# GpSimd's gathers of edge rows no longer wait for TensorE's sums of dense chunks

## The reference, cut to what matters

```python
# x (6250, 64) f32, src/dst/edge_type_32 (200000,) i32, edge_weight (200000,) f32
h_src = x[src]                                    # layer 0: 32 relation types over 4 bases
msg = einsum('ebo,eb->eo', einsum('ei,bio->ebo', h_src, weight), w_comp[etype]) * edge_weight[:, None]
x1 = layernorm(x + relu(segment_sum(msg, dst, 6250) + bias0))
# layer 1: self loops of weight 1, each edge scaled by 1 / (sum of weights at its destination)
norm = deg_inv[dst] * ew
y = segment_sum(norm[:, None] * (x1 @ W)[src], dst, 6250) + b
out = layernorm(x1 + y)
```

## Time and profile before

| | |
|---|---|
| three timed executions | 2766.74, 2771.0, 2766.0 us; median 2766.74 |
| profiled execution, first to last instruction (span) | 2042.2 us |
| profiled execution's own time around its span | not given by the page |
| median less span | 724.5 us |
| mean granted TensorE clock | 0.867 of full speed |
| busy, of the span | PE 73%, GpSimd 73%, VectorE 63%, ScalarE 42% |
| gathers (L824) | 1559, 947 ns each |

### The profile page before, as it was taken

How to read it: one execution, slowest core, us unless ns; L and a number is a source line. 1 busy time by engine, 2 the same in 40 slices (tenths; PEclk the granted TensorE clock), 3 DMA queues, 4 the chain that set the end, 5 groups by cost and what they waited for, 6 DMA issues and landing times.

```text
span 2042.2 us, 61156 instructions
## 1 busy us (share of the span) xinstructions
PE 1497.4 (73%) x21470; PEld 1196.1 (59%) x21470; DVE 1288.6 (63%) x3623; ACT 856.8 (42%) x2171; POOL 1495.6 (73%) x1590
## 2 busy tenths in 40 slices
PE   3785566655765776777677687778778788888986
PEld 2554444544554655566566566566667667677854
DVE  8886555756557555666655575565765656477647
ACT  5563343534444443444344344443444434344313
POOL 7777777777777777777777777777777777777750
PEclk7898777878787888888888898899999999899998
DMA  5544434434334455445444545554355554455695
GB/s 135 156 148 149 141 103 142 140 128 134 92 128 140 121 152 156 147 128 152 142 121 136 147 107 160 148 151 142 105 155 157 165 163 110 122 179 141 198 346 187
DMA packets 197569, 299.93 MB, mean 147 GB/s; under 512 B 66502, under 2 KB 137083, under 8 KB 191135
## 3 DMA queue, kind: packets, MB, share of 16 engines
q1 hardware_dynamic: 99496, 167.96, 23.3%
q0 software_dynamic: 50112, 51.41, 12.9%
q10 hardware_dynamic: 47671, 76.76, 12.4%
HBM read 187.43 MB, written 108.56 MB: 145 GB/s over the span
## 4 chain that ended last, share of the span: by engine, by line
PE 33%; POOL 29%; issue 19%; DMA 9%; DVE 3%; ACTq 3%; ACT 2%; DVEq 1%; POOLq 1%
POOL gathered_rows L824 29%; DMA gathered_rows<-in_x,idx 8%; PE coefs_ps L1383 4%; PE types_ps L1259 4%; PE coefs_ps L1349 3%; PE node_ps L1259 3%; PE sums_ps L1259 3%; PE sums_ps L1283 3%; PE dense_ps L1259 3%; PE sums_ps L1296 3%; ACTq L648 2%; ACT room L1056 1%; PE node_ps L1269 1%; PE sums_ps L1360 1%; PE coefs_ps L1244 1%
## 5 line engine op out<-in xcount | busy, mean ns | idle before, releaser
L824 POOL DMA_INDIRECT gathered_rows<-in_x,idx x1559 | 1475.7, 947 | 477.5 <-issue 426.7
L1283 PE MATMUL sums_ps<-gathered_rows,chunk_factors 128*32 128x64 f32 x3118 | 98.3, 253 | 407.0 <-DMA gathered_rows<-in_x,idx 218.7
L1897 DVE TENSOR_TENSOR first_room<-first_room,dve_ps 128x1024 bf16<-128x1024 bf16 x585 | 365.0, 679 | 0.0
L1283 PEld LDWEIGHTS sums_ps<-gathered_rows,chunk_factors 128*32 128x32 f32 x3118 | 63.1, 125 | 423.2 <-issue 208.6
L1056 ACT COPY room<-dense_ps 128x294 f32 x390 | 168.8, 433 | 332.1 <-PE dense_ps L1259 277.5
L985 ACT COPY parts<-sums_ps 128x128 f32<-128x128 f32 x196 | 52.0, 265 | 465.6 <-PE sums_ps L1283 462.3
L1919 DVE TENSOR_TENSOR dve_ps<-coefs_ps,edges 128x32 f32<-128x32 f32 x196 | 38.6, 197 | 330.7 <-PE coefs_ps L1244 326.2
L1259 PE MATMUL dense_ps<-first_room 128*128 128x245 bf16 x1170 | 219.2, 301 | 31.8 <-DVE first_room L1897 31.6
L1056 ACT COPY room<-node_ps 128x294 f32 x390 | 168.8, 433 | 168.1 <-PE node_ps L1259 61.8
L1891 DVE TENSOR_TENSOR first_room<-dve_ps,first_room 128x1960 bf16<-128x1960 f16 (+2 forms) x260 | 238.7, 939 | 0.0
L1259 PE MATMUL sums_ps<-first_room 128*128 128x245 bf16 (+1 forms) x1170 | 233.8, 312 | 0.0
(11 more groups left out here) (300 smaller groups left out, 2470.4 us busy)
## 6 DMA issues: line engine op xcount, KB each, us to landing
acc_room<-block_table ACTq DMA_DIRECT2D x147, 374.5 KB
block_table<-room SPq DMA_DIRECT2D x11, 2621.5 KB
type_rows<-in_edge_type SPq DMA_DIRECT2D x260, 96.0 KB
gathered_rows<-in_x,idx POOLq DMA_INDIRECT x1559
block_table<-room SPq DMA_DIRECT2D x9, 2247.0 KB
block_table<-room SPq DMA_DIRECT2D x9, 1872.5 KB
block_table<-room SPq DMA_DIRECT2D x10, 1498.0 KB
acc_room<-block_table ACTq DMA_DIRECT2D x43, 321.0 KB
```

What stands on the lines that cost most here:

```text
L824: pool.indirect_dma_start(gathered_rows[:, s, j, 0:D], None, rows, bass.IndirectOffsetOnAxis(ap=idx[:, s, j:j + 1], axis=0)).then_inc(rows ...
L1283: last = nc.tensor.matmul(parts_ps[lane:lane + LANE, D * k:D * k + D], chunk_factors[:, q, c, :], rows, start=True, stop=True)
L1897: last = nc.vector.tensor_tensor(lo_hot[:, w, q0:q1, :, :], lo_hot[:, 2, q0:q1, :, :], part_of_weights(w), ALU.mult)
```

## The change

The table of the awaited counts, the waits with their increments, and the parameter that turned them on go. Everything else stays, the wait for `idx_ready` at the head of each group too.

```diff
-GATHERED_BEHIND = {2: 5, 4: 8, 6: 9}
...
-assert 2 * FETCHES > FIRST_REGULAR + 1 and max(GATHERED_BEHIND.values()) <= 2 * CH
...
-        gathers_paced = sem("gathers_paced")
...
-            def gather_group(step, s, chunks, rows, behind_dense=False):
+            def gather_group(step, s, chunks, rows):
 
                 pool.wait_ge(idx_ready, step + 1)
 
                 pool.sem_inc(gathers_begun, 1)
                 for j in range(chunks):
-                    if behind_dense and j in GATHERED_BEHIND:
-                        pool.wait_ge(dense_summed, step * CH + (FREE_HOTS - CH + GATHERED_BEHIND[j]))
-                        pool.sem_inc(gathers_paced, 1)
                     pool.indirect_dma_start(gathered_rows[:, s, j, 0:D], None, rows,
...
-                        gather_iter(m, v, but_one if v == FETCHES - 1 else whole, True)
+                        gather_iter(m, v, but_one if v == FETCHES - 1 else whole)
...
-                        gather_group(i * U + s, s, CH, x[:, :], True)
+                        gather_group(i * U + s, s, CH, x[:, :])
```

More of the change, by code:

```diff
@@ L834, in _, with gather_iter @@
             with pool.If(early == 1):
-                def gather_iter(m, v, chunks, behind_dense=False):
+                def gather_iter(m, v, chunks):
                     for s in range(U):
-                        gather_group(m * (FETCHES * U) + (v * U + s), s, chunks[s], x[:, :], behind_dense)
+                        gather_group(m * (FETCHES * U) + (v * U + s), s, chunks[s], x[:, :])
                 whole, but_one = (CH, CH, CH), (CH, CH, CH - 1)
```

## The result

The changed kernel takes 3056.14 us (median of 4, 3053.12 to 3057.91), the kernel before 2766.55 us: ratio on record 1.1035, 95% interval 1.1015 to 1.1055 (the two medians alone give 1.105). The prediction said 2766.7 us and gave a tenth to everything outside 2761 to 2772 us. The profiled execution of the changed kernel takes 3057.1 us in all and its span is 3055.3 us, so only 1.8 us lie around the span.

The account below looks back on a forecast made before the run. The prediction took GpSimd's rate of gathers, one every 1.25 us, as the bound, with TensorE waiting for it. Its terms, 0 + 0 + 0 + 0, left the time at 2766.7 us, range 2761.0 to 2772.0.

Parts of the forecast that it names:

- the 724.5 us: Excess of the timed median, 2766.74 us, over the first profile's span, 2042.2 us; left unexplained.
- Slower TensorE work could make them hold: GpSimd's waits might hold in timed executions if TensorE ran slower inside the span; still priced at nothing.
- gathers that go earlier are merely early: If waits held, TensorE would be the bound, so releasing GpSimd's gathers sooner would change nothing: 0 us.
- Steps 1 to 3: GpSimd's 513 waits hold nothing, have time to spare, and their instructions hide in the gather gap: 0 us each.
- the 5.7 us to spare at the tightest place: Gather 1434, gather 6 of its group: its awaited dense chunks were done 5.7 us before it started.
- Step 3: Waits, increments and register arithmetic between GpSimd's gathers are covered by the 0.305 us gap: 0, at most 4.7 us gained.
- Step 4, contention,: GpSimd's gathers meeting VectorE's one-hot building: no stall in the rows, so no term, despite a rule allowing up to 679 ns.
- A: Faster: gaps named after TensorE are the waits' own, or waits hold when timed; 43.6 us gained, 2723.1 us, chance 0.06.
- B: Slower: gathers let loose collide with SyncE's dense block stores and land late; 19 us, 2785.5 us, chance 0.04.

Follow-up runs that it names:

- after_again: The changed kernel, unedited, run again beside the kernel before on a fifth chip: 2051.53 us, ratio 1.000 (0.999 to 1.001).
- met_waits: The kernel before with its 513 waits and increments kept, each wait for 24 dense chunks less, so always met: 3072.16 us, ratio 1.110.
- before_again: The kernel before, unedited, profiled once more: 2763.85 us, span 2758.5 us.
- drain_three: The changed kernel with gathers 3 and 6 of a group waiting for its earlier gathers' landing, iterations 8 to 64: 2966.19 us, ratio 1.073.
- cap_two: The changed kernel with gathers 2 to 7 each waiting for the landing of the gather two earlier, iterations 8 to 64: 2984.1 us, ratio 1.077.
- The drains: The changed kernel with waits for the group's own earlier landings before gathers 2, 4, 6 (3390.26 us) or 3, 6 (2966.19 us).
- spread_all: The kernel before with a wait in front of each of gathers 1 to 7 of a group instead of three: 2759.52 us, ratio 0.997.

## Why the prediction was wrong

**The step that failed** is in the sum, where the first profile stands in for the timed executions. "No view gives the profiled execution's own time outside its span, so I can't tell how much of the 724.5 us lies before the first and behind the last instruction", it says; 1.8 us do. The profile was of an execution of about 2044 us (2042.2 + 1.8), the times were of executions of 2767 us. Of the ways out that the prediction weighed, "Slower TensorE work could make them hold" was the right one, and the term put behind it, nothing, because "gathers that go earlier are merely early", was wrong by 290 us: gathers that go earlier slow TensorE down. No row of the first profile could price that, and no price was sought.

**Steps 1 to 3** (what the waits hold, how far they are from holding, what their instructions cost) are right for the execution that was profiled, and for its kind of chip: after_again gives 1.000. On the other kind the waits hold GpSimd for hundreds of us, and the 5.7 us to spare at the tightest place are gone. Step 3, no gain from dropping the instructions themselves, fits both within what can be told: on the 2047 kind nothing moves, and met_waits and the kernel after differ by 16 us (3072 and 3056 us), 0.5%, perhaps of different chips.

**Step 4, contention,** looked at whether VectorE slows GpSimd. The gathers' median stays at 942 to 947 ns in every kernel here, so that half is right, and no term was due. As a test of the rule of the Trainium skill that was cited there (SBUF — State Buffer, the trap of VectorE blocking GpSimd's DMAs) it says little: no row shows that VectorE's 679 ns operation runs in the two-port mode of which the rule speaks. The other direction, what the gathers do to TensorE, was never priced: the first profile showed next to nothing of it.

**Where the 296.8 us came from**, 3055.3 less 2758.5 of span, on TensorE's side: holes 784 - 446 = +338 us; busy time 2011.0 - 1849.5 = +161.5; long gaps 237 - 441 = -204; together 296. The busy time of the same instructions grew with the time at the lower of TensorE's two clock levels (1.2 against 2.4 GHz): a mean granted clock of 0.79 is 2 x 0.21 x 2758 = 1160 us at the lower one, 0.75 is 2 x 0.25 x 3055 = 1530 us. In the group before the one shown, the holes lasted from 1505.6 to 1512.9 us; the clock (the third column from the right) stood at the upper level from 1503 to 1509 and at the lower from 1510 to 1516, and the same three matmuls took 0.49 us in the one stretch and 0.80 us in the other:

```profile
1503.00:1509.00 6.00, 3.87 (x53) 1.00 0.15 31
1510.00:1516.00 6.00, 3.90 (x38) 0.50 0.26 62
```

```profile
1503.54 0.49 PE L1253 MATMUL types_ps<-first_room 128*128 128x245 bf16 x3
...
1513.53 0.80 PE L1253 MATMUL types_ps<-first_room 128*128 128x245 bf16 x3
```

So the clock fell while TensorE stood in holes; whether the holes made it fall was not tried by itself.

**Why the waits help there.** Share of the time spent in holes, by the place in its run of the gather that went out last (from the traces' lists, without the first 60 us and the tail):

```
gather of the run            1st   2nd   3rd   4th   5th   6th   7th   8th   1.3-2.5 us after the last   2.5-4 us
after (3055)                 .09   .03   .05   .34   .55   .53   .59   .59   .50                         .05
before_again (2758)          .06   .08   .10   .25   .39   .39   .49   .38   .25                         .05
drain_three                  .02   .01   .03   .08   .17   .50   .51   .49   .15                         .04
cap_two                      .03   .02   .04   .10   .48   .50   .52   .43   .05                         .01
before, first profile (2042)  9th and later: .03
```

The holes set in with the fourth or fifth gather of an unbroken run and stop when the last has landed. A wait that holds ends a run early. In drain_three from the 6th column on, and in cap_two from the 5th, the columns are almost all iterations 0 to 7, which have no waits (24 us a column).

It is not the number of gathers in flight. With a gather counted as in flight from its start to the end of its last packet, two are in flight for 1166 us of the kernel after and for 1155 us of cap_two; holes take 38% of the one and 4% of the other. With three or more in flight the share in the kernel after is no higher, 29% of 228 us. The mean number is 1.3 in the kernel after, 1.4 in cap_two, and 2.2 in after_again, which has the fewest holes of the three. What goes with the holes is a row of gathers that has gone on unbroken for 4 to 5 us, on the 2767 kind only. The drains and cap_two agree with that, as far as their long gaps let them tell. That breaking the rows pays in time is shown only by the kernel before and its variants, whose waits come when TensorE has got on.

**Rivals.** A was wrong in sign: waits hold in the timed executions, as its condition said, and taking them away costs. B, with a chance of 0.04, had sign and condition ("the eight go out as soon as idx is there") but the wrong mechanism: it priced late landings (3.3 us each, 19 us in all), and what the burst delays is TensorE's own instructions, at some 2.0 us for each group of the 171 ((784 - 446) / 171).

**Open.** Why TensorE stands still is not settled. The matmuls between the holes wait for nothing that the trace shows and take no longer than others, and they start at steps of about 0.71 us or twice that. It looks as if TensorE came by its instructions slowly while gathers go on, living for 4 to 5 us on those it has, but no run measured that supply. The recorded transfers of the page's instruction queue q8 don't show it: 173 of them in the kernel after and 174 in after_again, 0.99 and 1.06 us long in the median; how long one was awaited isn't recorded. Whether GpSimd's part of a gather or its transfer disturbs was not separated either, but from 1.3 to 2.5 us after the start of a run's last gather, with which GpSimd is through after 0.94 us, holes still take half of the time. Nor is it known what makes a chip of the one kind or the other. With no wait for TensorE holding, the 2047 kind has 58 to 71 us of holes (six profiles) and the 2767 kind 784, and landings are no later on the latter (the median last packet 2.1 us after the start in the kernel after, 2.4 us in after_again). No kernel with all its gathers beat the one before by more than the 0.3% of spread_all.

## What to carry to other kernels

When the span of a profile and the timed median lie far apart, as the 724.5 us here, the profile may be of another regime: take a second one before reading a wait as idle. A wait that never holds in a trace may still be what keeps bursts of gathers short where another engine suffers from them; judge it by a run with the wait always met, against one as it is. And price a freed engine's traffic on every other engine, not just its own gain.

## What the runs showed of the hardware

- On three chips unbroken rows of gathers of 128 rows, one every 1.25 us, went with holes of 0.3 to 1.1 us in TensorE's work: the same 21470 matmuls span 1674 us without gathers and 3055 us with them, 784 us of it holes. In six profiles on chips of the other kind the holes are 58 to 71 us with the gathers going out more densely.
- It was the same with 64 bytes a row as with 256 (3056.57 and 3056.14 us), and with x in another buffer (3054.45 us).
- The number of gathers in flight did not matter: with two in flight, 38% of the time was holes in the kernel after and 4% in cap_two.
- Three dense matmuls took 0.49 us at a granted clock of 1.00 and 0.80 us at 0.50.
- Increments of a semaphore on GpSimd, 78 ns each, ran under the gather before, six of them in front of every gather or twelve in front of every second; sixteen in front of each gather made the period 1.73 us, nineteen 1.96 us, against 1.25 us.
